# An eight-layer transformer kernel: int8 layer by halves, first steps of the deformable loop reordered, a position split on VectorE, last expert's sums in other PSUM banks

## The chip, the cores and the metric

The kernel runs on one core of a Trainium2 chip. The metric is the device time of one execution in microseconds (us), taken as the median over several executions. The core has TensorE (PE in the profile; PEld is its weight load), VectorE (DVE), ScalarE (ACT), GpSimd (POOL) and SyncE (SP), which issues DMAs. The engines run side by side and meet at semaphores: an instruction can wait for a count, and an instruction can add to one when it has finished. Each engine executes its own instructions in program order. PSUM has 8 banks of 512 fp32 columns on 128 partitions.

## The reference

The input `x` is 16 x 64 tokens of 128 features. Eight residual layers follow each other, each `x = x + layer(layernorm(x))`:

```python
x = x + L0_xattn(...)      # attention over the context, 16 heads
x = x + L0_ffn(...)        # 8 routed and 2 shared SwiGLU experts
x = x + L1_xattn(...)      # channel attention, twice
x = x + L1_ffn(...)        # int8 linear: round(x / x_scale) @ weight_q.T, scaled back, + bias
x = x + L2_xattn(...)      # deformable attention: 5 sampled points for each of 16 heads
x = x + L2_ffn(...)        # 8 experts, 512 wide, top 2, on the first 512 tokens
x = x + L3_xattn(...)      # attention with mask and bias
x = x + L3_ffn(...)        # quantised SwiGLU
```

Three of them matter here. The int8 linear:

```python
x_scale = jnp.maximum(amax, 1e-6) / 127.0
x_q = jnp.clip(jnp.round(x2d / x_scale), -128, 127).astype(jnp.int8)
acc = dot(x_q, weight_q.T)
return acc * x_scale * weight_scale[None, :]     # then + bias
```

The deformable attention computes a position `ix` for each query, head and point (an offset from a linear layer, wrapped by a modulus, rescaled), reads keys and values at `floor(ix)` and `floor(ix) + 1` with weights `1 - dx` and `dx`, and attends over the five points. The expert layer is `h = gelu(x w1[e])`, `y = h w2[e]`, added to each of its tokens with the gate weight of expert e.

## The kernel before, in words

Activations are kept with the tokens on the partitions (`x_tm`, 8 tiles of 128 tokens) and, for matmuls, with the features on the partitions (`h_fm`). Every engine's program is written out by hand, in the order of the calls; nothing reorders it.

**Int8 layer** (`int8_linear`, L1338 on). VectorE first casts the int8 weights and an identity matrix to bf16 (`wq8b`, `ident_b`, L1356, L1357), takes the row maxima of the normed `h_tm`, scales and rounds all 8 tiles, and clips them in one instruction (L1364). TensorE transposes the 8 tiles into bank 4 (L1398), ScalarE copies the whole bank to SBUF (L1424), and TensorE multiplies (L1404). Its result lies in bank 2 (tiles 0 to 3) and bank 3 (tiles 4 to 7). VectorE multiplies each half by the row scales (L1369), by the weight scales (L1374), adds it to `x_tm` (L1375) and takes the statistics of the next layernorm, which is done by halves too (`HalfNorm`: `moments`, `root` on ScalarE, `factors`, then two of four tiles on VectorE and two on ScalarE, `turn` on TensorE, `keep_turned` on ScalarE). Behind the int8 matmuls TensorE has other work in its order: nine transposes of the last layer's weights (L1411), the keys of the last attention (L1415), and fillers (`stay_busy`, L242: matmuls whose result nobody reads), and only then `first_norm.turn`.

**Deformable layer** (`deformable`, L1446 on). TensorE makes queries and offsets for each half. `positions` (L1609 on) turns offsets to positions on 256 columns at a time, and then splits each fp32 position into three bf16 parts (L1636 to L1640), which a one-hot bf16 matmul can move without loss. VectorE does the first of the four blocks, GpSimd the other three one after another. A *unit* is one of four groups of heads in one of two halves of the tokens: 8 units. For each unit `move` (TensorE, 3 matmuls into bank 3) and `keep_positions` (ScalarE) place the positions. Then ten `broadcast`s (two matmuls each, L1744) fill banks 0, 1, 2 in turn; blocks 1, 4 and 7 go to ScalarE (`ramp`, L1833, then `other_side`, L1839) and the other seven to VectorE (`near`, L1906), which writes interpolation weights ("hats"). A broadcast waits until the block three before it has been read. The loop runs over steps w = 0 to 17, two to a unit: `sample(w)` (16 matmuls, L1758) applies the hats of unit w // 2 to keys and values, `to_sbuf` (ScalarE, L1849) copies that out, `turn` (TensorE, L1769) turns it, VectorE multiplies and adds up; `turn_edge` (L1569) and `keep_edge` make the mask of the window's end. During the steps of one unit the hats of the next are made. `spread_q` (ScalarE, L1825) prepares the queries. Ahead of step 0 VectorE also runs `bound_last_keys`, three instructions on the keys of the last attention (L1308 to L1310).

**Experts** (`experts_and_last_attention`). For each expert `up` makes 4 banks of hidden values in banks 0 to 2 in turn, ScalarE applies gelu (L2493), `down(e)` (L2119, 32 matmuls with weight loads) sums into bank 3, and VectorE adds it to `x_tm` with the gate (L2336). Bank 3 is free again after that, so `down(e)` waits for `sum_added`. The last expert uses a bank per tile, in the order 3, 0, 1, 2, and VectorE adds them one at a time (L2347). Then the layernorm of tiles 0 to 3 starts (`late_rows`), with fillers on TensorE ahead of its turn (L367), and its queries go through `guard_queries` (L1289 on) on VectorE before TensorE may start `scores(4)`.

Of the kernel before, what the change touches and what calls it, by code (L numbers as in the profile page):

```python
# [20 lines left out]
P = 128  # L21
B, S, D = 16, 64, 128
T = B * S
NT = T // P
# [91 lines left out]
def build(nc, A, out):  # L116

    ctx = ExitStack()
    with ctx:
# [1042 lines left out]
        def channel_attention(n):  # L1162
# [60 lines left out]
            def _(dve):  # L1223
# [15 lines left out]
                dve.wait_ge(dve_chain, biased)  # L1239
                for k in range(2):  # L1240
# [27 lines left out]
        channel_attention(2)  # L1268

        wq8b = sb("wq8b", [P, P], BF16)
        ident_b = sb("ident_b", [P, P], BF16)

# [28 lines left out]
        def bound_last_keys(dve):  # L1304
# [3 lines left out]
            V.tensor_scalar(nonf, k_fm[:], 0.0, 0.0, ALU.mult, ALU.not_equal)  # L1308
            V.tensor_scalar(h_fm[:], k_fm[:], 0.0, 1e4, ALU.max, ALU.min)
# [28 lines left out]
        def int8_linear(n):  # L1338
# [15 lines left out]
            def _(dve):  # L1354
                dve.wait_ge(rest_in, REST)
                V.tensor_copy(wq8b[:], wq8[:])  # L1356
                V.tensor_copy(ident_b[:], ident)  # L1357
# [27 lines left out]
            def _(pe):  # L1385
                tp = ps[:, 4, :].bitcast(BF16)

# [58 lines left out]
        def deformable(n):  # L1446
            s = lambda name: sem(f"def_{name}")
            q_ps, q_sb, qt_ps, qt_ok, qx_ok = s("q_ps"), s("q_sb"), s("qt_ps"), s("qt"), s("qx")
            off_ps, parts_ok, parts1_ok, mv_ps, ix_ok = s("off_ps"), s("parts0"), s("parts1"), s("moved_ps"), s("ix")
# [85 lines left out]

            MOVE_STEPS = (None, 0, 1, 3, 5, 7, 9, 11)

            def moved(u):  # L1540

# [1351 lines left out]
```

## Time and profile before

| | us |
|---|---|
| median of 3 runs | 464.21 (463.15 to 467.38) |
| the profiled execution, its own time | 463.37 |
| its span, first to last instruction | 461.6 |

| engine | busy us | share of the span | instructions |
|---|---|---|---|
| TensorE | 398.0 | 86% | 3415 |
| VectorE | 359.8 | 78% | 802 |
| ScalarE | 253.0 | 55% | 438 |
| GpSimd | 114.5 | 25% | 97 |

The mean granted clock of TensorE was 0.974 of its full 2.4 GHz. The span lies between the first and the last instruction; the 1.8 us between it and the execution's own time lie around it. A timeline row gives the start, the time taken from the first start to the last end of a group, the engine, the line, the operation with its names and shapes, the count, and, in brackets, how long the engine sat idle before it and what ended that. Instructions of one engine overlap a little, so the start of the next tells more of the pace than the end of the last.

### The profile page before, as it was taken

What the parts mean: (1) busy time and instruction counts of PE and PEld (TensorE: products, weight loads), DVE (VectorE), ACT (ScalarE), POOL (GpSimd) and SP (SyncE); (2) the same over time, 40 slices, a digit from 0 to 9 for tenths busy, and PEclk for the clock granted to TensorE, in tenths of its full rate; (3) what the DMA queues carried; (4) which work ended last, traced back from release to release, by engine and by line L of the source; (5) the groups of instructions that cost most, each with busy time, mean ns of one, the idle gap of its engine ahead of it and who ended that gap; (6) DMA issues with size and microseconds to landing.
All of it is one profiled execution on the core that took longest, in us unless ns stands there. A gap on an engine that the chain in (4) does not pass through costs nothing.

```text
span 461.6 us, 8687 instructions
## 1 busy us (share of the span) xinstructions
PE 398.0 (86%) x3415; PEld 262.4 (57%) x3415; DVE 359.8 (78%) x802; ACT 253.0 (55%) x438; POOL 114.5 (25%) x97
## 2 busy tenths in 40 slices
PE   8988989999999988786787888899999999868156
PEld 5555566566666667553454546385556766643045
DVE  4799646558544587979879898999899689988985
ACT  4785753333223334456797784766766433444942
POOL 3200000006990001005995544031221023100200
PEclk9999999999999999989999999999999999989759
DMA  7890000000000000017000003000000000000001
GB/s 227 357 322 6 1 1 1 1 0 1 0 1 0 1 3 2 0 58 309 2 1 0 3 1 70 0 2 0 2 0 3 1 1 3 1 0 0 1 1 45
DMA packets 11084, 16.51 MB, mean 36 GB/s; under 512 B 5274, under 2 KB 9764, under 8 KB 10148
## 3 DMA queue, kind: packets, MB, share of 16 engines
q1 hardware_dynamic: 10756, 15.17, 9.4%
q10 hardware_dynamic: 288, 0.79, 0.6%
q8 instruction: 27, 0.44, 0.4%
q14 instruction: 13, 0.11, 0.1%
HBM read 15.43 MB, written 0.52 MB: 35 GB/s over the span
## 4 chain that ended last, share of the span: by engine, by line
PE 48%; DVE 32%; ACT 11%; issue 7%; DMA 1%; POOL 0%; ACTq 0%; DVEq 0%
PE ps L852 7%; PE ps L857 7%; PE ps L891 7%; PE ps L2119 4%; PE ps L2109 2%; PE ps L242 2%; DVE arena L1906 2%; DVE stats L252 2%; PE ps L1758 2%; PE ps L2146 1%; DVE arena L610 1%; DVE arena L613 1%; PE ps L2662 1%; DMA ctx_fm<-in_ctx_fm 1%; PE ps L2643 1%
## 5 line engine op out<-in xcount | busy, mean ns | idle before, releaser
L970 DVE SCALAR_TENSOR_TENSOR arena<-ps,cols,arena 128x512 f32<-128x512 f32 x40 | 29.7, 750 | 42.3 <-PE ps L857 38.0
L866 ACT ACTIVATE arena<-ps,cols 128x512 f32<-128x512 f32 x40 | 27.4, 687 | 63.9 <-PE ps L852 63.8
L242 PE MATMUL ps<-const 128*128 128x256 f32 x162 | 43.0, 412 | 7.4 <-ACT arena L2709 4.4
L891 PEld LDWEIGHTS ps<-weights,arena 128*128 128x128 f32 x320 | 38.6, 192 | 8.1 <-issue 8.0
L1906 DVE TENSOR_SCALAR arena<-ps 128x512 f32<-128x512 f32 x56 | 36.4, 683 | 7.3 <-PE ps L1744 3.5
L242 PEld LDWEIGHTS ps<-const 128*128 128x128 f32 x162 | 31.4, 203 | 16.3 <-ACT arena L2709 4.7
L891 PE MATMUL ps<-weights,arena 128*128 128x128 f32 x320 | 39.2, 276 | 0.2 <-DVE x_tm L959 0.2
L857 PE MATMUL ps<-h_fm,weights 128*128 128x512 f32 x80 | 37.7, 593 | 0.7 <-DVE arena L970 0.7
L852 PE MATMUL ps<-h_fm,weights 128*128 128x512 f32 x80 | 37.7, 594 | 0.6 <-ACT h_fm L373 0.6
L2109 PE MATMUL ps<-h_fm,weights 128*128 128x512 f32 x64 | 30.3, 606 | 2.7 <-ACT arena L2493 1.8
L1744 PE MATMUL ps<-l2buf,picks_b 128*128 128x256 bf16 x160 | 25.5, 275 | 6.5 <-DVE arena L1906 4.7
L2119 PEld LDWEIGHTS ps<-weights,arena 128*128 128x128 f32 x256 | 29.4, 192 | 2.6 <-issue 2.6
L2119 PE MATMUL ps<-weights,arena 128*128 128x128 f32 x256 | 30.0, 275 | 0.9 <-DVE x_tm L2336 0.9
L857 PEld LDWEIGHTS ps<-h_fm,weights 128*128 128x128 f32 x80 | 15.1, 190 | 20.2 <-issue 18.2
L1758 PE MATMUL ps<-arena,kexp 128*32 128x320 f32 x256 | 20.5, 438 | 5.3 <-ACT l2buf L1849 3.9
L1065 POOL TENSOR_TENSOR wn<-wn,winv 128x1152 f32<-128x1152 f32 x1 | 2.1, 2129 | 85.7 <-DVE winv L1055 85.7
L2493 ACT ACTIVATE arena<-ps 128x512 f32<-128x512 f32 x32 | 18.0, 597 | 9.2 <-PE ps L2109 9.1
L959 DVE SCALAR_TENSOR_TENSOR x_tm<-ps,arena,x_tm 128x128 f32<-128x128 f32 x80 | 22.4, 342 | 0.3 <-DVE stats L252 0.2
L1744 PEld LDWEIGHTS ps<-l2buf,picks_b 128*128 128x128 bf16 x160 | 12.6, 99 | 17.0 <-DVE arena L1906 10.0
L2109 PEld LDWEIGHTS ps<-h_fm,weights 128*128 128x128 f32 x64 | 11.2, 189 | 17.7 <-issue 10.2
L852 PEld LDWEIGHTS ps<-h_fm,weights 128*128 128x128 f32 x80 | 13.7, 191 | 10.4 <-issue 9.6
L2275 POOL TENSOR_TENSOR arena<-arena 128x1024 f32<-128x1024 f32 x5 | 11.5, 2301 | 31.6 <-DVE arena L2374 31.6
(401 smaller groups left out, 890.8 us busy)
## 6 DMA issues: line engine op xcount, KB each, us to landing
weights<-in_moe_w SPq DMA_DIRECT2D x2, 2048.0 KB, 10.0
weights<-in_moe_w SPq DMA_DIRECT2D x3, 1280.0 KB
l2buf<-in_picks SPq DMA_DIRECT2D x1, 1664.0 KB, 7.9
rows<-in_rows SPq DMA_DIRECT2D x1, 1024.0 KB, 13.7
x_tm<-in_x SPq DMA_DIRECT2D x2, 256.0 KB, 5.2
ctx_fm<-in_ctx_fm ACTq DMA_DIRECT2D x1, 512.0 KB, 5.9
ctx_tm<-in_ctx SPq DMA_DIRECT2D x1, 512.0 KB, 14.5
mats<-in_mats SPq DMA_DIRECT2D x1, 512.0 KB, 14.8
```

The costliest lines, as they stand in the source:

```text
L242: PE.matmul(ps[:, bank, 0:256], ident, const[:, 0:256], start=True, stop=True)
L852: PE.matmul(ps[:, k, :], w1[:, e, P * k:P * k + P], h_fm[:, t], start=True, stop=True)\
L857: PE.matmul(ps[:, 2 + k, :], w2[:, e, P * k:P * k + P], h_fm[:, t], start=True, stop=True)\
L866: AC.activation(silu[:, k, :], ps[:, k, :], ACT.Silu, bias=bias_col(0, e, k)).then_inc(silu_ok, 1)
L891: ins = PE.matmul(ps[:, 4 + u % 2, P * t:P * t + P], glu[:, u % 2, k, P * t:P * t + P], w3[:, e, k, :], start=(k == 0), stop=(k == 1))
L959: ins = V.scalar_tensor_tensor(out=x_tm[:, j], in0=ps[:, 4 + u % 2, P * t:P * t + P], scalar=gates[:, j, e:e + 1], in1=x_tm[:, j], op0=ALU ...
L970: V.scalar_tensor_tensor(out=glu[:, u % 2, k, :], in0=ps[:, 2 + k, :], scalar=bias_col(1, e, k), in1=silu[:, k, :], op0=ALU.add, op1=ALU.m ...
L1744: ins = PE.matmul(ps[:, m % 3, 256 * i:256 * i + 256], picks_b[:, 2 * c + i, :], ixm[:, hg, 256 * half:256 * half + 256], start=True, stop ...
L1758: ins = PE.matmul(ps[32 * hl:32 * hl + 32, 4 + par, 0:NK * S], kvc[:, j, 4 * hg + hl, :], hats[:, u % 2, NK * hl:NK * hl + NK, S * (2 * i ...
L1906: V.tensor_scalar(hat_rows(u, c), ps[:, m % 3, :], 0.0, 1.0, ALU.max, ALU.min).then_inc(near_ok, 1)
L2109: PE.matmul(ps[:, n % 3, :], m2w1[:, e, P * k:P * k + P], h_fm[:, 0:T2], start=True, stop=True)\
L2119: ins = PE.matmul(at_ps, hid[:, e % 2, k, P * j:P * j + P], m2w2[:, e, k, :], start=(k == 0), stop=(k == 3))
```

## The change

1. **Casts.** The casts to `wq8b` and `ident_b` move from the head of the int8 layer into the channel attention ahead of it, in front of VectorE's wait for that layer's result.
2. **Int8 by halves.** The clip, the transposes (now banks 4 and 5), the copy and the waits go by halves of four tiles. The row scales of the second half are applied by ScalarE, in four instructions of one tile each, straight from bank 3.
3. **Table.** The exponential that makes ScalarE load its table moves from behind `keep_positions(0)` to between `keep_turned` and `keep_queries(1)` of the second half.
4. **First steps.** The block-to-bank turn starts at bank 2 instead of 0, with the waits to match. The `move` of unit 1 comes after broadcast 2 (before: in step 0), the `move` of unit 2 inside step 1 before its last two broadcasts (before: at its end). In step 0 the first three broadcasts of the next unit come before `sample(0)`, and `spread_q(0)` after that step's ramps.
5. **Split.** GpSimd computes the third unit's positions but doesn't split them; VectorE splits them at the end of step 0 (new `split_positions`, the five instructions cut out of `positions`).
6. **Last keys.** `bound_last_keys` leaves the place ahead of step 0. Its first instruction goes to the end of step 2, the other two to the end of step 3.
7. **Last expert.** The banks per tile go 0, 1, 2, 3, so only the fourth tile waits for the sum before. The filler ahead of `late_rows.turn` shrinks from 4 to 2.

The diff, cut to its core:

```diff
+                V.tensor_copy(wq8b[:], wq8[:])
+                V.tensor_copy(ident_b[:], ident)
                 for k in range(2):
                     t = slice(4 * k, 4 * k + 4)
                     dve.wait_ge(y_ps, k + 1)
...
-                V.tensor_scalar(xq, t, -128.0, 127.0, ALU.max, ALU.min).then_inc(xq_ok, 1)
+                for k in range(2):
+                    r = slice(4 * k, 4 * k + 4)
+                    V.tensor_scalar(xq[:, r], t[:, r], -128.0, 127.0, ALU.max, ALU.min).then_inc(xq_ok, 1)
...
-                    dve.wait_ge(y_ps, k + 1)
-                    dve_link(V.tensor_tensor(y[:, r], ps[:, 2 + k, :].rearrange("p (j c) -> p j c", j=4),
-                                             over(xs[:, r], 2, D), ALU.mult))
+                    if k == 0:
+                        dve.wait_ge(y_ps, 1)
+                        dve_link(V.tensor_tensor(y[:, r], ps[:, 2, :].rearrange("p (j c) -> p j c", j=4),
+                                                 over(xs[:, r], 2, D), ALU.mult))
                     if k == 1:
                         first_norm.factors(dve)
                         first_norm.apply_on_dve(dve, (0, 1))
+                        dve.wait_ge(xT_ok, 6)
...
-                pe.wait_ge(xq_ok, 1)
-                for j in range(NT):
-                    ins = PE.transpose(tp[:, P * j:P * j + P], xq[:, j], ident_b[:])
-                ins.then_inc(xT_ps, 1)
-                pe.wait_ge(xT_ok, 1)
                 for k in range(2):
+                    pe.wait_ge(xq_ok, k + 1)
+                    tp = ps[:, 4 + k, :].bitcast(BF16)
+                    for j in range(4):
+                        ins = PE.transpose(tp[:, P * j:P * j + P], xq[:, 4 * k + j], ident_b[:])
+                    ins.then_inc(xT_ps, 1)
+                for k in range(2):
+                    pe.wait_ge(xT_ok, k + 1)
...
-                act.wait_ge(xT_ps, 1)
-                AC.activation(xT, ps[:, 4, :].bitcast(BF16), ACT.Copy).then_inc(xT_ok, 1)
+                for k in range(2):
+                    act.wait_ge(xT_ps, k + 1)
+                    AC.activation(xT[:, 512 * k:512 * k + 512], ps[:, 4 + k, :].bitcast(BF16)[:, 0:512], ACT.Copy)\
+                        .then_inc(xT_ok, 1)
+                act.wait_ge(y_ps, 2)
+                for j in range(4, NT):
+                    AC.activation(y[:, j], ps[:, 3, P * (j - 4):P * (j - 4) + P], ACT.Copy, scale=xs[:, j:j + 1])\
+                        .then_inc(xT_ok, 1)
...
                 second_norm.keep_turned(act, 4)
+                AC.activation(warm, const[:, C_BIAS1:C_BIAS1 + 1], ACT.Exp)
                 keep_queries(1)
...
-            MOVE_STEPS = (None, 0, 1, 3, 5, 7, 9, 11)
+            MOVE_STEPS = (None, None, 1, 3, 5, 7, 9, 11)
...
-                positions(pool, G, pool_link, 1, slice(0, 4), parts1_ok)
-                positions(pool, G, pool_link, 0, slice(4, 8), parts1_ok)
-                positions(pool, G, pool_link, 1, slice(4, 8), parts1_ok)
+                positions(pool, G, pool_link, 1, slice(0, 4))
+                for g in range(2):
+                    positions(pool, G, pool_link, g, slice(4, 8))
+                    split_positions(G, pool_link, g, slice(4, 8), parts1_ok)
...
                 for c in range(10):
-                    if c < 2:
-                        pe.wait_ge(qt_ok, c + 1)
+                    if c == 0:
+                        pe.wait_ge(off_sb, 4)
+                    if c in (1, 2):
+                        pe.wait_ge(qt_ok, c)
+                    broadcast(0, c)
                     if c == 2:
-                        pe.wait_ge(off_sb, 4)
-                    broadcast(0, c)
+                        move(pe, 1)
...
-                    if w == 0:
-                        sample(0)
                     if w % 2 == 0 and chunks(w):
                         pe.wait_ge(ix_ok, w // 2 + 2)
                     for c in chunks(w)[:3]:
                         broadcast(w // 2 + 1, c)
+                    if w == 0:
+                        sample(0)
+                    if w == 1:
+                        move(pe, 2)
...
-                bound_last_keys(dve)
...
+                    if w == 0:
+                        dve.wait_ge(third_raw, 1)
+                        split_positions(V, dve_link, 1, slice(0, 4), third_ok)
...
+                    if w == 2:
+                        find_last_keys(dve)
+                    if w == 3:
+                        bound_last_keys(dve)
...
-            SUM_BANK, LAST_BANKS = 3, (3, 0, 1, 2)
+            SUM_BANK, LAST_BANKS = 3, (0, 1, 2, 3)
...
-                    if e >= 1:
-                        pe.wait_ge(sum_added, e)
                     for j in range(4):
+                        if e >= 1 and (j == 3 if e == NE - 1 else j == 0):
+                            pe.wait_ge(sum_added, e)
...
-                stay_busy(pe, 4, 2)
+                stay_busy(pe, 2, 2)
                 late_rows.turn(pe, 0)
```

## Rows read from the trace of the kernel before

**Rows 1.** Page, part 4: the chain that ended last, shares by engine.
```profile
PE 48%; DVE 32%; ACT 11%; issue 7%; DMA 1%; POOL 0%; ACTq 0%; DVEq 0%
```

**Rows 2.** Windows: stretch, busy us (count) by engine, granted clock, DMA.
```profile
197.20:200.70 3.50, 3.50 (x12) 2.47 (x11) 3.33 (x13) 1.45 (x4) 0.00 (x0) 0.51 0.03 7
```

**Rows 3.** Timeline of VectorE, channel attention to int8 layer; columns as explained above.
```profile
182.60 1.40 DVE L1246 TENSOR_TENSOR x_tm<-x_tm,ps 64x512 f32<-64x512 f32 x2 [2.38 <-PE ps L1216]
...
190.12 0.22 DVE L1356 CAST wq8b<-wq 128x128 bf16<-128x128 int32 x1
...
194.07 0.69 DVE L1364 TENSOR_SCALAR arena<-arena 128x1024 bf16<-128x1024 f32 x1
...
197.06 0.69 DVE L1369 TENSOR_TENSOR arena<-ps,arena 128x512 f32<-128x512 f32 x1 [1.16 <-PE ps L1404]
```

**Rows 4.** Timeline of TensorE, int8 layer.
```profile
196.56 0.62 PE L1404 MATMUL ps<-wq8b,arena 128*128 128x128 bf16 x8 [1.12 <-ACT arena L1424]
...
198.75 2.81 PE L1415 MATMUL ps<-ctx_fm,mats 128*128 128x512 f32 x4
...
202.70 0.66 PE L367 MATMUL ps<-const,h_tm 128*128 128x128 f32 x4 [0.27 <-ACT h_tm L349]
```

**Rows 5.** Timeline of ScalarE, int8 layer to the first ramps.
```profile
195.48 1.02 ACT L1424 ACTIVATE arena<-ps 128x1024 bf16<-128x1024 bf16 x1 [2.57 <-PE ps L1398]
...
201.77 0.88 ACT L349 ACTIVATE h_tm<-x_tm,shift,rstd 128x128 f32<-128x128 f32 x2 [0.22 <-DVE shift L341]
...
209.13 0.60 ACT L373 ACTIVATE h_fm<-ps 128x512 f32<-128x512 f32 x1 [0.75 <-PE ps L367]
210.94 0.69 ACT L1592 ACTIVATE q_fm<-ps,cols 128x512 f32<-128x512 f32 x1 [1.22 <-PE ps L1501]
...
213.81 1.28 ACT L1861 ACT_TABLE_LOAD   x1
```

**Rows 6.** Timeline of VectorE, first steps of the deformable loop.
```profile
218.90 0.82 DVE L1308 TENSOR_SCALAR wn<-k_fm 128x1024 int32<-128x1024 f32 x1
...
220.65 1.22 DVE L1310 TENSOR_SCALAR q_fm<-k_fm 128x1024 f32<-128x1024 f32 x1
...
225.98 1.63 DVE L1971 TENSOR_TENSOR x_tm<-x_tm,rows 128x1024 f32<-128x1024 f32 x1
...
237.31 0.69 DVE L1906 TENSOR_SCALAR arena<-ps 128x512 f32<-128x512 f32 x1 [1.31 <-PE ps L1744]
```

**Rows 7.** Timeline of TensorE, first steps of the deformable loop.
```profile
219.93 1.28 PE L1758 MATMUL ps<-arena,kexp 128*32 128x320 f32 x16 [1.37 <-ACT arena L1839]
...
225.72 1.28 PE L1758 MATMUL ps<-arena,kexp 128*32 128x320 f32 x16 [0.42 <-ACT l2buf L1849]
...
228.01 0.67 PE L1569 MATMUL ps<-const,o_fm 128*128 128x80 f32 x4 [0.56 <-ACT l2buf L1586]
```

**Rows 8.** Timelines: the split on VectorE (first, last of five), GpSimd's position steps.
```profile
210.77 0.29 DVE L1636 CAST l2buf<-o_fm 128x256 bf16<-128x256 f32 x1
...
212.09 0.43 DVE L1640 TENSOR_TENSOR l2buf<-o_fm,l2buf 128x256 bf16<-128x256 f32 x1
...
220.25 1.06 POOL L1634 TENSOR_TENSOR ctx_tm<-ctx_tm 128x256 f32<-128x256 f32 x1
...
226.62 1.94 POOL L1623 TENSOR_SCALAR o_fm<-o_fm 128x256 f32<-128x256 f32 x1
```

**Rows 9.** Timelines of ScalarE, VectorE and TensorE around the last expert.
```profile
368.77 0.88 ACT L349 ACTIVATE h_tm<-x_tm,shift,rstd 128x128 f32<-128x128 f32 x2 [0.44 <-DVE shift L341]
...
374.00 0.43 DVE L1289 TENSOR_SCALAR arena<-q_fm 128x512 int32<-128x512 f32 x1 [0.60 <-ACT q_fm L2498]
...
362.77 3.81 PE L2119 MATMUL ps<-weights,arena 128*128 128x128 f32 x32 [0.93 <-DVE x_tm L2336]
...
368.93 1.99 PE L242 MATMUL ps<-const 128*128 128x256 f32 x8
370.76 0.60 PE L367 MATMUL ps<-const,h_tm 128*128 128x128 f32 x4
```

More of the change, by code:

```diff
@@ L1302, in build, with find_last_keys @@
         keys_bounded = []
-        def bound_last_keys(dve):
+        def find_last_keys(dve):
             dve.wait_ge(l3_keys[1], 2)
@@ L1308, in bound_last_keys @@
             V.tensor_scalar(nonf, k_fm[:], 0.0, 0.0, ALU.mult, ALU.not_equal)
+        def bound_last_keys(dve):
             V.tensor_scalar(h_fm[:], k_fm[:], 0.0, 1e4, ALU.max, ALU.min)
@@ L1543, in moved, with wait_parts @@
                 return hg, slice(256 * half, 256 * half + 256)
+            def wait_parts(pe, n):
+                if n == 1:
+                    pe.wait_ge(third_ok, 1)
+                else:
+                    pe.wait_ge(parts1_ok, n - 1)
             def move(pe, u):
                 hg, c = moved(u)
-                edges = sum(step < MOVE_STEPS[u] for step in EDGE_STEPS) if u else 0
+                edges = sum(step < MOVE_STEPS[u] for step in EDGE_STEPS) if u >= 2 else 0
                 if edges:
@@ L1562, in turn_edge @@
             def turn_edge(pe, g):
-                pe.wait_ge(ix_ok, 1 + sum(step < EDGE_STEPS[g] for step in MOVE_STEPS[1:]))
+                pe.wait_ge(ix_ok, 2 + sum(step < EDGE_STEPS[g] for step in MOVE_STEPS[2:]))
                 if g >= 1:
-                    pe.wait_ge(parts1_ok, g)
+                    wait_parts(pe, g)
                 for i in range(2):
@@ L1605, in _, with positions @@
                 second_norm.keep_turned(act, 4)
+                AC.activation(warm, const[:, C_BIAS1:C_BIAS1 + 1], ACT.Exp)
                 keep_queries(1)
                 keep_offsets(1)
-            def positions(eng, E, link, g, pairs, done):
+            def positions(eng, E, link, g, pairs):
                 c = slice(S * pairs.start, S * pairs.stop)
@@ L1633, in positions, with split_positions @@
                     link(E.tensor_tensor(jq(t), jq(t), st, ALU.mult))
-                    link(E.tensor_tensor(o, o, t, ALU.add))
+                    if g == 1 and pairs.start == 0:
+                        E.tensor_tensor(o, o, t, ALU.add).then_inc(third_raw, 1)
+                    else:
+                        link(E.tensor_tensor(o, o, t, ALU.add))
+            def split_positions(E, link, g, pairs, done):
+                c = slice(S * pairs.start, S * pairs.stop)
+                o, t = off[g][:, c], t1[g][:, c]
                 link(E.tensor_copy(parts[g][:, 0, c], o))
@@ L1680, in _ @@
             def _(dve):
-                positions(dve, V, dve_link, 0, slice(0, 4), parts_ok)
+                positions(dve, V, dve_link, 0, slice(0, 4))
+                split_positions(V, dve_link, 0, slice(0, 4), parts_ok)
                 for k in range(2):
@@ L1743, in broadcast @@
                     for i in range(2):
-                        ins = PE.matmul(ps[:, m % 3, 256 * i:256 * i + 256], picks_b[:, 2 * c + i, :],
+                        ins = PE.matmul(ps[:, (m + 2) % 3, 256 * i:256 * i + 256], picks_b[:, 2 * c + i, :],
                                         ixm[:, hg, 256 * half:256 * half + 256], start=True, stop=True)
@@ L1775, in _ @@
                 for c in range(10):
[L1776 to L1777 removed]
+                    if c == 0:
[3 more added lines that the diff above has]
+                    broadcast(0, c)
                     if c == 2:
[L1779 to L1780 removed]
+                        move(pe, 1)
                 pe.wait_ge(kv_ok, 8)
                 for w in range(NW + 2):
[L1783 removed]
+                    if w in MOVE_STEPS[3:]:
                         move(pe, MOVE_STEPS.index(w))
@@ L1798, in _ @@
                         sample(w)
-                    if w == 1:
-                        move(pe, 2)
                     if w == 14:
@@ L1860, in _ @@
                 keep_positions(act, 0)
-                AC.activation(warm, const[:, C_BIAS1:C_BIAS1 + 1], ACT.Exp)
                 for c in ACT_BLOCKS:
                     ramp(0, c)
+                    if c == ACT_BLOCKS[0]:
+                        keep_positions(act, 1)
                 for c in ACT_BLOCKS:
@@ L1866, in _ @@
                 for w in range(NW + 2):
-                    if w in MOVE_STEPS[1:] and w != 1:
+                    if w in MOVE_STEPS[3:]:
                         keep_positions(act, MOVE_STEPS.index(w))
-                    if w == 0:
-                        spread_q(0)
                     if w in EDGE_STEPS:
```

21 lines of the change are left out of this document (10 added, 11 removed).

## The prediction

> **What bounds the kernel now.** I read the page's chain first, then the timelines of each engine over the three places the diff touches, then the windows for the granted clock. By the chain TensorE sets 48% of the span, VectorE 32%, ScalarE 11%, DMA 1% [rows 1]: no engine bounds the whole, it is a relay. So an edit is worth what it takes out of the handoffs on the chain at its place, and everything behind a shortened handoff moves forward as one, as long as nothing from outside (a DMA, GpSimd) is met. I therefore follow one mark through each place: how much earlier does it happen?
>
> **Casts and clip.** The two casts stand between `h_tm` and the row maxima. The first starts at 190.12 [rows 3] and the pair held VectorE up by about 0.15. In the channel attention VectorE sits idle 2.38 ahead of 182.60 [rows 3], so 0.4 of casts is covered there; without that cover it would cost its 0.4. Behind L1246 nothing else waits for them. The clip of 1024 columns takes 0.69 [rows 3]; half of that plus a fixed part is about 0.42, so the first half is ready 0.27 sooner.
>
> **Int8 relay.** The copy of the whole bank on ScalarE takes 1.02 [rows 5]; 512 columns take 0.60 (L373 [rows 5]), 0.42 less. The eight matmuls or transposes take 0.62 [rows 4] at a pace of 0.06, so four transposes are done 0.23 sooner. Sum for L1369 of the first half: 0.15 + 0.27 + 0.23 + 0.42 = 1.07 earlier, 196.0 instead of 197.06. The second half follows 0.5 behind on ScalarE, and its four scalings are new: two instructions of 128 columns with two operands from memory take 0.88 (L349 [rows 5]), so four take 1.7. They run from about 196.4 to 198.1, while VectorE still adds the first half, and the weight copies behind them on ScalarE still finish by 199.6, when the `root` is wanted. On VectorE they save 0.7. By VectorE and ScalarE alone the normed half would be ready 1.3 earlier.
>
> TensorE is what is late next. Its fixed work (L1411, L1415, fillers) starts behind the last int8 matmul: 196.0 + 0.23 instead of 196.56 + 0.45, which is 0.78 earlier, and it ended 0.27 before `first_norm.turn` [rows 4]. So the turn comes 0.78 + 0.27 = 1.05 earlier: **1.05** is the gain of this part.
>
> The clock bears on it. From 197.2 to 200.7 the granted clock was 0.51, the lower level of 1.2 GHz, after TensorE had been idle for 1.12 of the time just before [rows 2, 4]; the four passes of L1415 took 2.81. With halves TensorE waits less there. If the clock stays up, TensorE is ready over 1 us sooner and the turn is bound by ScalarE, at 1.3 instead of 1.05. I take 1.05 and keep 0.25 for the range.
>
> **Table load.** The load takes 1.28 at 213.81 [rows 5], ahead of the first ramp. Its new place is the 1.22 in which ScalarE waits before L1592 [rows 5]. With the warm exponential it overhangs by 0.2, and TensorE's own queries cover that. It takes about 0.7 off the first ramp, which else waits for its broadcast. The Trainium skill (ScalarE: Activation LUTs, What ACT_TABLE_LOAD costs) adds a drain of 1.38 us to the load; by that the overhang would be 1.6 and nearly all the benefit gone, but here the next instruction starts right behind the 1.28.
>
> **First steps.** I walked the ten broadcasts, the seven hats (about 0.61 apart) and the three ramps forward by their waits, starting 1.0 earlier than before. ScalarE's `other_side`s end at 218.3, so `sample(0)` starts at 218.35 against 219.93 [rows 7]: 1.6 earlier. VectorE has no `bound_last_keys` ahead of step 0; it ran from 218.90 to about 221.8 [rows 6], 2.8 of work, in front of the hats that `sample(1)`'s banks waited for. With three broadcasts ahead of `sample(0)` only the fourth hat waits, till about 220.0. Then comes the split: the five instructions took 1.75, 210.77 to 212.52 [rows 8], and the raw positions are there in time: GpSimd starts 1.05 earlier, and its add ended at 221.31 [rows 8], so 220.3 at the latest.
>
> What does the split cost beside a busy GpSimd? The trace has VectorE instructions on SBUF at that time: 1024 columns take 0.82 and 1.22 [rows 6] where 0.69 is normal [rows 3], 1.4 times on average. Lower bound: 1.75. Upper: each of the five waits for one GpSimd step, 1.94 the longest [rows 8]. I take 1.4 times, 2.4. This is the rule of the Trainium skill that speaks against the change (SBUF — State Buffer, SBUF: two separate sides): VectorE and GpSimd take turns at one pair of ports, and who comes second stands still for the whole instruction; its worst is rival D.
>
> Behind the split wait the hats of step 1, `move(2)` and broadcasts 18 and 19. Walked on: the last of these hats starts at about 224.8, `sample(1)` at 224.5 against 225.72, and, since `move(2)` no longer stands between it and the edge, `turn_edge(0)` at 225.8 against 228.01 [rows 7]. That is **2.2 earlier**, 1.05 of which came from the int8 layer. x_tm's bias add (L1971, 1.63 [rows 6]) then ends at about 227.1, in time for the multiply that waits for the turn behind broadcast 20.
>
> **Last keys.** The first instruction (0.8) at the end of step 2 falls into waits of VectorE and delays two hats by 0.2, with no effect on `sample(3)`, which waits for ScalarE. The other two (2.1) at the end of step 3 meet an idle of 1.31 before 237.31 [rows 6], so the next hat is 1.0 late with the 0.2. Its broadcast successor has 0.5 of slack; `sample(4)` gets 0.5 later. From there VectorE is tight, so it stays: **0.5 back**. The bounds are 0 and the whole 2.9. The loop leaves 2.2 - 0.5 = **1.7** earlier. GpSimd, rid of one split, is further ahead of need than before, and no DMA bounds the loop (1% of the chain [rows 1]).
>
> **Last expert.** `down(7)` waited 0.93 for the sum before it [rows 9]. Three of its tiles need not; the fourth comes long after it. The whole tail is 0.93 earlier. Then the layernorm: TensorE did four fillers from 368.93 to 370.76 [rows 9], 0.46 each, and the normed tiles were there at 368.77 + 0.88 = 369.65 [rows 9], so the filler held up the turn. With two it is at 368.93 - 0.93 + 0.92 = 368.92, 1.84 earlier. The guard on VectorE started at 374.00 after an idle of 0.60 [rows 9]; its own queue allows 0.93 + 0.60 less a gap, so **1.5** earlier. `scores(4)` waits for that guard. Nothing on the way to the end is bound from outside.
>
> **Sum.** 1.7 + 1.5 = 3.2. The profiled execution took 463.37, so 460.2 by its own account. The median of the runs is 464.21, 0.84 above; the same 3.2 from it gives **461.0** (0.7% less). One per cent is 4.6 us, and that is what a measurement of this kernel can tell from no change.
>
> **Rivals.**
> *A, as summed:* 461.0, chance 0.50. Its own range is 459.9 to 462.0.
> *B, the clock stays up and the ports hardly meet:* 0.25 more in the int8 layer, 0.65 for the split, and 0.5 if the two last-key instructions are hidden wholly, 1.4 in all: 459.6; with the four passes of L1415 and the loop's dense start a little less again, 459.0. For it: idle of TensorE shrinks [rows 4], GpSimd's steps are short beside VectorE's. Against: 0.82 and 1.22 in the rows [rows 6]. Chance 0.27.
> *C, the moved work is paid in full:* the last keys cost 2.9 instead of 0.5, because VectorE has no slack once the start is tight: 2.4 back, 463.4. Against: the idle of 1.31 [rows 6]. Chance 0.15.
> *D, slower:* the split queues behind GpSimd at each step. GpSimd then runs the first steps of its next block, with the 1.94 among them [rows 8]. If the five together take 1.75 + 5 x 1.0 = 6.8 instead of 2.4, 4.4 are lost: 465.4. It decides from a split of 5.6 on, where the 3.2 are gone. At five times 1.94, 11.5 for the split, it would be 470.1. The rule named above is this one at its worst. Against: the 0.82 and 1.22 of the two instructions [rows 6] are at most 0.53 over normal. Chance 0.08.
>
> **How the numbers follow.** The range takes A and B, and of C all but its end: 459.0 to 463.4. Faster by over 1% means under 459.6: B's greater part and the low end of A, 0.28. Slower by over 1% means over 468.8, only the far end of D and what I overlooked: 0.05. The rest, 0.67, is within 1%.
>
> **What would show it.** Right: L1369 near 196.0 and the first turn (L367) near 201.7; no table load ahead of the first ramp; `sample(0)` near 218.4, `turn_edge(0)` near 225.8; the split under 3; VectorE without idle ahead of the first hat of step 4; `down(7)` without wait, the second-last turn near 368.9 less the loop's gain, and the guard 1.5 earlier beyond the loop's gain. Wrong: a split over 4, idle of VectorE ahead of it (raw positions late), `sample(4)` less than 1 earlier than before, or TensorE at 0.5 of its clock in a stretch of the loop where it was at 1.00.

## The result, and the profile after

The kernel after takes **461.32 us** (median of 20 runs, 459.6 to 466.37); the kernel before, run beside it, 466.04 (20 runs, 463.15 to 469.25). The ratio is 0.9907, with a 95% interval of 0.988 to 0.9933. The predicted 461.0 us is close, but part of that is cancellation: one step failed, and two terms, the int8 layer and the tail, were larger than I made them. A ratio below leaves out executions more than 1.5% above the fastest of their own kernel, which takes 5 of the 12 of parts 1 to 6 and 3 of the 12 of the loop with fillers and none elsewhere; medians and mean clocks are of all executions. The ratios follow the means more than the medians, so they are not the quotients of the medians shown. The profiled execution of after took 460.47, span 458.4, so 2.9 and 3.2 less than that of before.

The marks of the prediction, as starts in the two traces (us):

| mark | before | after | distance from the mark above: before, after |
|---|---|---|---|
| `x_tm` add of the channel attention | 182.60 | 182.32 | |
| first turn of the normed half (L367) | 202.70 | 201.11 | 20.10, 18.79 |
| `sample(0)` | 219.93 | 217.96 | 17.23, 16.85 |
| `sample(1)` | 225.72 | 224.11 | 5.79, 6.15 |
| `turn_edge(0)` | 228.01 | 226.29 | 2.29, 2.18 |
| `sample(4)` | 238.95 | 238.25 | 10.94, 11.96 |
| `keep_last_values`, behind the loop | 291.60 | 290.66 | 52.65, 52.41 |
| `down(7)` | 362.77 | 360.72 | 71.17, 70.06 |
| its layernorm's turn (L367) | 370.76 | 367.79 | 7.99, 7.07 |
| guard of the queries (L1289) | 374.00 | 371.20 | 3.24, 3.41 |
| end of the span | 461.6 | 458.4 | 87.60, 87.20 |

So between the two traces the int8 layer gives 1.31, the deformable loop from the turn to `keep_last_values` takes back 0.65 (88.90 to 89.55), and the tail gives 1.86. The rest, 0.28 ahead of the first changed line and 0.40 behind the guard, lies where nothing was changed.

The chain of after, from the page, against [rows 1]: still a relay, no engine carries it alone.

```profile
PE 47%; DVE 34%; ACT 10%; issue 7%; DMA 1%; POOL 0%; ACTq 0%; DVEq 0%
```

**Int8 layer.** Timeline of VectorE after; L1366, L1372 are the L1364, L1369 of [rows 3]:

```profile
179.93 0.18 DVE L1241 CAST wq8b<-wq 128x128 bf16<-128x128 int32 x1
...
182.32 0.68 DVE L1249 TENSOR_TENSOR x_tm<-x_tm,ps 64x512 f32<-64x512 f32 x1 [2.07 <-PE ps L1216]
...
193.73 0.77 DVE L1366 TENSOR_SCALAR arena<-arena 128x512 bf16<-128x512 f32 x2
...
195.81 0.69 DVE L1372 TENSOR_TENSOR arena<-ps,arena 128x512 f32<-128x512 f32 x1 [0.18 <-PE ps L1408]
```

Timelines of ScalarE and TensorE after, against [rows 4, 5]:

```profile
194.65 1.08 ACT L1429 ACTIVATE arena<-ps 128x512 bf16<-128x512 bf16 x2 [2.02 <-PE ps L1402]
196.22 1.15 ACT L1433 ACTIVATE arena<-ps,arena 128x128 f32<-128x128 f32 x4 [0.49 <-PE ps L1408]
...
195.30 0.88 PE L1408 MATMUL ps<-wq8b,arena 128*128 128x128 bf16 x8 [0.35 <-ACT arena L1429]
...
197.01 1.88 PE L1419 MATMUL ps<-ctx_fm,mats 128*128 128x512 f32 x4
...
201.11 0.66 PE L367 MATMUL ps<-const,h_tm 128*128 128x128 f32 x4 [1.35 <-ACT h_tm L349]
```

The casts sit in an idle that is still 2.07 long. The first half comes nearly as predicted: L1372 at 195.81 where 196.0 was forecast, and 0.97 earlier behind the `x_tm` add, where 1.07 was. TensorE has less idle (0.35 where [rows 4] had 1.12), its four passes take 1.88 and not 2.81, and it now waits 1.35 for ScalarE ahead of the turn.

**First steps of the loop.** Timeline of TensorE after, against [rows 7]: steps 0 and 1.

```profile
217.96 1.28 PE L1786 MATMUL ps<-arena,kexp 128*32 128x320 f32 x16 [0.43 <-ACT arena L1869]
...
222.68 0.49 PE L1574 MATMUL ps<-v,picks_b 128*128 128x256 bf16 x3 [1.72 <-DVE v L1666]
...
224.11 2.25 PE L1786 MATMUL ps<-arena,kexp 128*32 128x320 f32 x16
226.29 1.15 PE L1587 MATMUL ps<-const,o_fm 128*128 128x80 f32 x4
```

`move(2)` (L1574) waits 1.72 for the split on VectorE. The `sample(1)` behind it takes 2.25 where `sample(0)` took 1.28. The windows (stretch, busy us and count of TensorE, its weight loads, VectorE, ScalarE, GpSimd, then granted clock and DMA) say why:

```profile
220.00:224.00 4.00, 1.70 (x12) 0.76 (x11) 3.90 (x9) 4.00 (x8) 3.59 (x6) 1.00 0.00 0
224.00:228.00 4.00, 4.00 (x27) 2.15 (x26) 2.12 (x4) 1.46 (x4) 3.84 (x4) 0.57 0.02 4
```

The granted clock is 0.57 from 224 to 228, mostly at the lower level of 1.2 GHz, behind 4 us in which TensorE was busy for 1.70. In before it was 1.00 over this stretch and low in the int8 layer instead [rows 2].

The split, timeline of VectorE after, against [rows 8]:

```profile
220.21 0.28 DVE L1662 CAST v<-ctx_tm 128x256 bf16<-128x256 f32 x1
220.53 0.50 DVE L1663 TENSOR_TENSOR ctx_tm<-ctx_tm,v 128x256 f32<-128x256 f32 x1
...
221.81 0.72 DVE L1666 TENSOR_TENSOR v<-ctx_tm,v 128x256 bf16<-128x256 f32 x1
```

From 220.21 to 222.53 are 2.32, forecast 2.4. No idle stands ahead of it (its row has no bracket): the raw positions are there in time.

The last keys, timeline of VectorE after, against [rows 6]:

```profile
234.90 1.02 DVE L1312 TENSOR_SCALAR h_fm<-k_fm 128x1024 f32<-128x1024 f32 x1
235.84 1.21 DVE L1313 TENSOR_SCALAR q_fm<-k_fm 128x1024 f32<-128x1024 f32 x1
236.97 0.68 DVE L1937 TENSOR_SCALAR arena<-ps 128x512 f32<-128x512 f32 x1
```

The 1.31 of idle ahead of the hat in [rows 6] is filled.

**Last expert.** Timeline of TensorE after, against [rows 9]: `down(7)`, the two fillers (four matmuls; the four of before were eight), the turn.

```profile
360.72 3.74 PE L2156 MATMUL ps<-weights,arena 128*128 128x128 f32 x32
...
366.82 1.13 PE L242 MATMUL ps<-const 128*128 128x256 f32 x4
367.79 0.60 PE L367 MATMUL ps<-const,h_tm 128*128 128x128 f32 x4
```

`down(7)` has no wait where [rows 9] had 0.93.

### The profile page after: what moved, and what is told of

It is laid out like the page before. It is cut to its first block, busy times and chain, and to the rows that moved or that the text cites. A ratio compares the mean times of both kernels' runs of the same rounds, so it can differ in the third digit from the quotient of the medians.

```text
span 458.4 us, 8682 instructions
## 1 busy us (share of the span) xinstructions
PE 396.8 (87%) x3411; PEld 260.9 (57%) x3411; DVE 360.2 (79%) x807; ACT 253.6 (55%) x443; POOL 111.7 (24%) x92
## 4 chain that ended last, share of the span: by engine, by line
PE 47%; DVE 34%; ACT 10%; issue 7%; DMA 1%; POOL 0%; ACTq 0%; DVEq 0%
PE ps L852 7%; PE ps L857 7%; PE ps L891 7%; PE ps L2156 5%; DVE arena L1937 3%; PE ps L2146 2%; PE ps L1786 2%; DVE stats L252 2%; DVE arena L2405 1%; DVE arena L2402 1%; DVE arena L610 1%; DVE arena L613 1%; PE ps L242 1%; DMA ctx_fm<-in_ctx_fm 1%; DVE arena L2433 1%
## 5 line engine op out<-in xcount | busy, mean ns | idle before, releaser
L1786 PE MATMUL ps<-arena,kexp 128*32 128x320 f32 x256 | 21.5, 455 | 3.7 <-ACT l2buf L1879 2.6
L2530 ACT ACTIVATE arena<-ps 128x512 f32<-128x512 f32 x32 | 18.0, 597 | 9.2 <-PE ps L2146 9.1
L1863 ACT ACTIVATE arena<-ps 128x512 f32<-128x512 f32 x24 | 14.4, 599 | 8.8 <-PE ps L1772 8.8
```

Of the source, the lines that this page charges most:

```text
L1786: ins = PE.matmul(ps[32 * hl:32 * hl + 32, 4 + par, 0:NK * S], kvc[:, j, 4 * hg + hl, :], hats[:, u % 2, NK * hl:NK * hl + NK, S * (2 * i ...
```

## Experiments

What is to be settled: whether the terms have the sizes that the prediction gave them; whether the wait for the split and the low clock behind it are what the loop lost; and whether GpSimd lengthens the split. The rival to the second is that the last keys (rival C) or the new order itself cost the loop its gain. In the lists below, the distance from the `x_tm` add to `keep_last_values`, the int8 layer and the loop together, is called the **front**: 109.00 in before, 108.34 in after.

### The tail alone

The kernel before, with part 7 of the change (and, in the second run, its banks without the shorter filler):

```diff
-            SUM_BANK, LAST_BANKS = 3, (3, 0, 1, 2)
+            SUM_BANK, LAST_BANKS = 3, (0, 1, 2, 3)
...
-                stay_busy(pe, 4, 2)
+                stay_busy(pe, 2, 2)
```

> The kernel before with part 7 alone (banks 0, 1, 2, 3 for the last expert, 2 fillers instead of 4). Theory (the two waits in the tail add up, as the two traces show them): the last expert starts 0.9 to 1.1 earlier, the guard behind the layernorm 1.5 to 1.9 earlier; 1.7 us faster, ratio 0.996. Rival (the tail is bound by something that comes back later, such as a low granted clock once there are fewer fillers): under 0.5 us.

> The kernel before with the new banks for the last expert, all 4 fillers kept. Theory: the sum's wait is worth 0.93 to 1.1 us by itself and the two fillers the other 0.6 to 0.8, so about 1.0 us faster. Rival: the turn is set by ScalarE and the fillers cost nothing, so the same as with 2 fillers, 1.7 us.

Whole part: ratio 0.996 (0.9929 to 0.999), median 463.39. Banks alone: 0.9978 (0.9947 to 1.001), median 465.08. The kernel before, in the series of this and the next two sections, had a median of 464.21 and a mean of 465.36 (35 runs), so for the banks alone the timing shows no gain. TensorE in the trace of the whole part, with VectorE's guard, then TensorE with the banks alone (without its `down(7)`, at 365.78):

```profile
361.63 3.74 PE L2119 MATMUL ps<-weights,arena 128*128 128x128 f32 x32
...
367.72 1.13 PE L242 MATMUL ps<-const 128*128 128x256 f32 x4
368.69 0.60 PE L367 MATMUL ps<-const,h_tm 128*128 128x128 f32 x4
...
372.10 0.42 DVE L1289 TENSOR_SCALAR arena<-q_fm 128x512 int32<-128x512 f32 x1
```

```profile
371.87 1.99 PE L242 MATMUL ps<-const 128*128 128x256 f32 x8
373.70 0.60 PE L367 MATMUL ps<-const,h_tm 128*128 128x128 f32 x4
```

From `down(7)` to the turn it is 7.06 with two fillers and 7.92 with four, 7.99 in before. From `keep_last_values` to the guard: 82.40 before, 80.55 with the part (361.63, 368.69 and the guard at 372.10, `keep_last_values` at 291.57), 81.22 with the banks alone. So the part is worth **1.85**, 1.18 of it the banks. The turn gains 0.86 by two fillers less, but the guard only 0.67: it starts 3.41 behind the turn instead of 3.24, and the idle of 0.60 ahead of it [rows 9] is gone, so now VectorE's own queue holds it. The 1.85 agrees with the timed 0.4% (1.9 us).

### The int8 layer alone

The kernel before, with parts 1 and 2 of the change (casts, halves):

> The kernel before with the casts moved and the int8 layer by halves (parts 1 and 2). Theory: the first turn of the layernorm comes 1.05 us earlier at the low granted clock, 1.3 with the clock up, and all of it is carried to the end: 1.0 to 1.3 us faster. Rival (the low clock only moves to a later stretch, where TensorE is on the path): 0 to 0.5 us.

Ratio 0.9985 (0.9955 to 1.0015), median 464.27. In the trace the first turn comes 18.79 behind the `x_tm` add, against 20.10: **1.31** earlier, and the front is 107.66, so 1.34 shorter, with nothing lost on the way to `keep_last_values`. Whether it reaches the end is not shown: the timing can't resolve 1.3 us (0.28%), and in this trace the stretch behind the guard is 1.4 longer than in before. The distance was 20.08 to 20.10 in each of the five traces without this part and 18.78 or 18.79 in each of the nine with it, whatever the rest of the kernel did. The clock's part is told by the banks-only kernel above, whose int8 layer is that of before and lies 4.2 later in its trace. The window that answers to [rows 2] there:

```profile
201.40:204.90 3.50, 3.50 (x17) 2.12 (x15) 3.33 (x13) 1.34 (x4) 0.00 (x0) 1.00 0.02 7
```

The clock was 1.00 where before had 0.51, and the distance was 20.08 all the same. The low clock of [rows 2] cost nothing, since VectorE and ScalarE set the turn.

### The loop alone

The kernel before, with parts 3 to 6 of the change (table, first steps, split, last keys):

> The kernel before with parts 3 to 6 (table, first steps, split, last keys). By my prediction the loop's share is 2.2 - 1.05 - 0.5 = 0.65 us faster. Theory of the moved clock stretch: in the trace after, TensorE fell to 0.5 of its clock at 224 to 227.6 us, behind an idle of 1.7 us that the split causes; without the int8 part the phase differs, so between 0.3 slower and 1.5 faster. Rival (VectorE is the bound of the loop): no gain, whatever the clock.

Ratio **1.0044** (1.0012 to 1.0076), median 466.76 against 464.21: slower, where my sum said 0.65 gained. TensorE in steps 0 and 1, then the window behind it:

```profile
219.38 1.28 PE L1779 MATMUL ps<-arena,kexp 128*32 128x320 f32 x16 [0.44 <-ACT arena L1862]
...
224.10 0.59 PE L1567 MATMUL ps<-v,picks_b 128*128 128x256 bf16 x3 [1.71 <-DVE v L1659]
...
225.74 2.26 PE L1779 MATMUL ps<-arena,kexp 128*32 128x320 f32 x16
```

```profile
224.00:228.00 4.00, 3.90 (x24) 1.16 (x24) 3.63 (x5) 2.36 (x5) 3.75 (x5) 0.57 0.02 4
```

The same idle and the same clock as in after. The front is 109.67, 0.67 longer, though `sample(0)` comes 0.38 sooner behind the turn. `sample(1)` then follows 6.36 behind it instead of 5.79, which takes that back, and between `turn_edge(0)` and `sample(4)` another 0.89 goes, to the last keys in this trace. Their two bounds on VectorE:

```profile
236.36 1.18 DVE L1312 TENSOR_SCALAR h_fm<-k_fm 128x1024 f32<-128x1024 f32 x1
237.46 1.10 DVE L1313 TENSOR_SCALAR q_fm<-k_fm 128x1024 f32<-128x1024 f32 x1
```

### Fillers in step 1, GpSimd made to wait, and both

Two edits to the kernel after: three fillers (six matmuls) ahead of `move(2)`, so that TensorE works while the split runs; and GpSimd kept from its next block of positions until the split has ended.

```diff
                     if w == 1:
+                        stay_busy(pe, 3, 7)
                         move(pe, 2)
...
                 positions(pool, G, pool_link, 1, slice(0, 4))
+                pool.wait_ge(third_ok, 1)
```

> The changed kernel with 3 fillers on TensorE in step 1, ahead of move(2), where it stood idle for 1.72 us; nothing else differs. Theory (the idle lowers the granted clock in the stretch behind it in most executions, which costs 1 to 1.8 us there): the stretch at 224 to 228 us shows a granted clock of 1.00, turn_edge(0) comes about 1 us earlier than in the trace after, and the ratio falls by 0.002 to 0.004 below that of the changed kernel (0.9907). Rival (the clock there costs nothing, because VectorE is what the loop waits for): the same 0.9907.

> The changed kernel with GpSimd waiting until VectorE has finished the split, before it starts its next block. Theory (the split's 2.3 us instead of 1.75 come from GpSimd working at the same time): the split takes 1.7 to 1.8 us, everything up to sample(1) is 0.4 to 0.5 us earlier, GpSimd's later blocks end 2.5 to 3 us later and nobody waits for them; 0.3 to 0.5 us faster. Rival (the split is slow because of its own chain or of ScalarE): it stays at 2.3 us and nothing changes.

> Both: 3 fillers in step 1 and GpSimd waiting for the split. If both theories hold, 1.3 to 2 us faster than the changed kernel: ratio 0.987. The fillers (1.5 us) might then be longer than the shortened idle (1.2 us), which would give 0.3 back.

The fillers: 0.9878 (0.9841 to 0.9915), median 460.46. TensorE in their trace:

```profile
220.97 1.46 PE L242 MATMUL ps<-const 128*128 128x256 f32 x6
222.85 0.49 PE L1574 MATMUL ps<-v,picks_b 128*128 128x256 bf16 x3 [0.41 <-DVE v L1666]
...
224.28 1.28 PE L1786 MATMUL ps<-arena,kexp 128*32 128x320 f32 x16
225.50 0.67 PE L1587 MATMUL ps<-const,o_fm 128*128 128x80 f32 x4
```

`move(2)` starts where it started (4.72 behind `sample(0)` in both), for the split is as long, but the idle is 0.41, `sample(1)` takes 1.28 and the edge comes 1.22 behind it instead of 2.18. The front is 106.33, 2.0 shorter than in after. About half of that, 0.96, is won ahead of the edge. Another 1.02 comes between the edge and `sample(4)` (10.94, 11.96 in after): 0.67 ahead of the first hat of step 2, and 0.35 because the two bounds on the last keys took 0.74 and 0.88 there, not 1.02 and 1.21.

GpSimd's wait: 0.9888 (0.9842 to 0.9934), median 460.46. VectorE in its trace, then TensorE:

```profile
221.92 0.28 DVE L1662 CAST v<-ctx_tm 128x256 bf16<-128x256 f32 x1
222.24 0.42 DVE L1663 TENSOR_TENSOR ctx_tm<-ctx_tm,v 128x256 f32<-128x256 f32 x1
...
223.22 0.42 DVE L1666 TENSOR_TENSOR v<-ctx_tm,v 128x256 bf16<-128x256 f32 x1
...
223.79 0.49 PE L1574 MATMUL ps<-v,picks_b 128*128 128x256 bf16 x3 [1.13 <-DVE v L1666]
```

The split takes **1.72** (221.92 to 223.64), the lower bound of the prediction (1.75), and the clock stays at 1.00 behind an idle of 1.13. Here another stretch was low, 0.58 from 208 to 212, ahead of the first hat: the way from the second turn to that hat took 7.45, against 5.95 in after. That puts the front at 107.55.

Both: 0.9866 (0.9834 to 0.9899), median 459.68. Its window over the disputed stretch:

```profile
224.00:228.00 4.00, 3.76 (x37) 2.30 (x35) 3.44 (x5) 3.39 (x8) 3.73 (x4) 1.00 0.00 0
```

The front is 106.07, 2.93 shorter than before and 2.27 shorter than after: the whole loss of the loop is gone, and 1.6 are won there. The median is the lowest of all, beside 465.4 of before in this series. But the intervals of all three versions overlap that of after (0.988 to 0.9933), so the timing doesn't show a gain over it.

### The last keys

The kernel after, with all three instructions on the last keys on 64 of 1024 columns. It leaves out the bounds of the other 960, so it is not a replacement:

```diff
-            V.tensor_scalar(h_fm[:], k_fm[:], 0.0, 1e4, ALU.max, ALU.min)
+            V.tensor_scalar(h_fm[:, 0:64], k_fm[:, 0:64], 0.0, 1e4, ALU.max, ALU.min)
```

> The changed kernel with the three instructions of the last keys' bounds on 64 instead of 1024 columns (left out: the bounds of the other 960, so this part of the keys' guard is not computed), which takes their 2.9 us nearly away. Theory (VectorE has slack at the end of step 2 and 1.3 of slack at the end of step 3): 0.5 us faster than the changed kernel. Rival C of the prediction (the moved work is paid in full): 2.4 us faster. Other rival (all hidden): no change.

Ratio 0.9932 (0.9899 to 0.9966), median 461.99: no gain over after. Timeline of VectorE:

```profile
236.71 0.30 DVE L1312 TENSOR_SCALAR h_fm<-k_fm 128x64 f32<-128x64 f32 x1
236.94 0.18 DVE L1313 TENSOR_SCALAR q_fm<-k_fm 128x64 f32<-128x64 f32 x1
238.16 0.69 DVE L1937 TENSOR_SCALAR arena<-ps 128x512 f32<-128x512 f32 x1 [1.05 <-PE ps L1772]
```

The time saved turns into 1.05 of idle ahead of the same hat. From the first hat of step 2 to `sample(4)` it is 9.96, as in before and with the fillers; in after it is 10.31 and in the loop alone 10.84. So the last keys cost nothing where their two instructions ran at 0.74 and 0.88, 0.35 where they took 1.02 and 1.21, and 0.88 in the loop alone, where the first of the three was long too (1.18). A second trace of after (below) has the same marks as this one up to this place, and its front is 109.68 against 109.70 here: in it the last keys, at 0.68 and 0.88, cost nothing. Rival C, with 2.9 in full, falls. Why the instructions are long in some traces was not tested by itself. This trace also repeats the low clock: 0.69 from 224 to 228.

### Do the parts add up?

The loop alone with the fillers; parts 1 to 6 of the change together; and, timed once more in the same series, the kernel after and the version with both edits:

> Parts 3 to 6 alone on the kernel before, with the 3 fillers in step 1. Parts 3 to 6 alone were 2.0 us slower (ratio 1.0044) at a mean granted clock of 0.963 instead of 0.967. Theory (the idle of TensorE in step 1 is the whole reason): the mean clock rises to 0.967 or more and the kernel is 0.7 to 1.5 us faster than before, ratio 0.997 to 0.9985. Rival (VectorE's new work, or something else in the order, makes the loop longer whatever the clock): it stays at 1.003 to 1.005.

> Parts 1 to 6 without part 7. Theory of a plain sum: 0.9907 of the whole less the 0.004 of the tail, so 0.9947. Theory that the parts don't add, as int8 alone (0.9985) and the loop alone (1.0044) give 1.003 together: 1.003.

> The changed kernel itself, on the chip and in the rounds of the others of this call: 0.9907 again within 0.003, mean granted clock 0.968.

> The changed kernel with fillers and with GpSimd waiting for the split, a second time: 0.9866 again within 0.003, 1.3 to 2 us under the changed kernel of this call. If it is within 0.5 us of the changed kernel, the first result was the spread between executions.

The kernel before stood at 466.77 here (23 runs, mean 466.23). The fourth column divides the mean of all executions by that mean.

| kernel | ratio (95%) | median us | ratio of all executions | mean granted clock |
|---|---|---|---|---|
| loop alone with fillers | 0.9974 (0.9933 to 1.0016) | 466.76 | 0.9998 | 0.965 |
| parts 1 to 6 | 0.994 (0.9901 to 0.9979) | 465.03 | 0.9991 | 0.965 |
| after | 0.9866 (0.9826 to 0.9905) | 460.79 | 0.9875 | 0.970 |
| after with both edits | 0.9871 (0.9832 to 0.991) | 460.87 | 0.9880 | 0.969 |

In the first two rows the two ratios differ, for the reason given with the result. By all executions both kernels are level with the kernel before, within about 0.004.

Two results went against me. The fillers did not make the loop alone faster than before; its traced execution (469.34, the longest of its 12) lost clock elsewhere, 0.70 from 208 to 212, and its front was 111.62. And the version with both edits did not beat after in this series, though its front was 106.05 in the trace, the same as in the first, while that of after was 109.68. VectorE and TensorE in this second trace of after:

```profile
221.82 0.54 DVE L1662 CAST v<-ctx_tm 128x256 bf16<-128x256 f32 x1
222.39 0.90 DVE L1663 TENSOR_TENSOR ctx_tm<-ctx_tm,v 128x256 f32<-128x256 f32 x1
...
224.79 0.49 PE L1574 MATMUL ps<-v,picks_b 128*128 128x256 bf16 x3 [2.22 <-DVE v L1666]
...
226.44 2.36 PE L1786 MATMUL ps<-arena,kexp 128*32 128x320 f32 x16
```

The split took 2.83 here and the idle was 2.22. The table sets the 14 traces side by side. The column "low clock at" tells where the granted clock of a 2 us window was under 0.95, in us behind the `x_tm` add; the windows cover 8 to 58 behind it. The trace of parts 1 to 6 is of the longest of its 12 executions too (469.3).

| traces | idle ahead of `move(2)` | split | second turn to first hat | low clock at | front |
|---|---|---|---|---|---|
| before, tail alone | none | | 5.84 | 14 to 18 | 109.00, 108.93 |
| banks alone, int8 alone | none | | 5.84 | nowhere | 108.91, 107.66 |
| after | 1.72 | 2.32 | 5.95 | 42 to 46 | 108.34 |
| loop alone | 1.71 | 2.33 | 5.95 | 14 to 18, 42 to 46 | 109.67 |
| after again, short last keys, parts 1 to 6 | 2.22 | 2.83 | 7.44 | 26 to 30, 42 to 48 | 109.68, 109.70, 109.88 |
| after with fillers | 0.41 | 2.31 | 5.95 | nowhere | 106.33 |
| after with GpSimd's wait | 1.13 | 1.72 | 7.45 | 26 to 30 | 107.55 |
| after with both, twice | none | 1.73 | 5.95 | nowhere | 106.07, 106.05 |
| loop alone with fillers | 0.93 | 2.83 | 7.45 | 22 to 26, 28 to 34 | 111.62 |

Three things are read from it. All five traces with the new first steps and neither edit have an idle of 1.7 or more ahead of `move(2)` and a low clock from 42 on; none of the five with an edit has either, nor the four with the old steps. That link is shown: the two edits touch the idle by different ways, and each takes the low clock away. A low clock at 26 to 30 goes with about 1.5 more ahead of the first hat, where TensorE has the queries, the offsets and the broadcasts in its order. (In the last row a low clock at 22 to 26 also goes with 7.34 instead of 5.74 from the first turn to the second.) And it carries on: GpSimd's block starts 28.68 behind the `x_tm` add in both traces of after, but the split starts 9.21 behind GpSimd in the first and 10.71 in the second, so it meets other steps of GpSimd. In all traces without GpSimd's wait it took 2.31 to 2.33 at 9.2 behind and 2.83 at 10.7.

What stays open is how much of it the median sees. Executions of one kernel differ by up to 8.5 us (6.8 for after), and the mean granted clock goes with it: after lay between 459.6 and 466.37, the slowest at a mean clock of 0.960, the traced one at 0.974. Further stretches behind the loop vary too: from the guard to the end it is 86.94 to 87.60 in nine traces and 88.10 to 88.97 in the other five. Six runs of each version don't separate a gain of 2 us from that. Nor is it settled whether the parts add: 0.9985 and 1.0044 give 1.003. Parts 1 to 6 together measured 0.994, which is 0.009 apart with about 0.006 of uncertainty on the difference, but by all executions 0.9991, which is 0.004 apart and within it. With the tail's 0.996 that would make 0.995 for the whole, where 0.9907 was measured, again within the uncertainty. Whether the int8 part changes how often the clock falls behind it was not tried.

## Why the prediction was right, and where it was wrong

**Int8 layer: mechanism right, 1.31 instead of 1.05.** The first half came within 0.1 of the forecast by its distance from the `x_tm` add. The step that was off is "TensorE is what is late next". The 0.27 of idle ahead of the turn in [rows 4] already said that TensorE was waiting for ScalarE in before, and with the clock at 1.00 it got there 1.35 early. So the figure for VectorE and ScalarE, 1.3, holds, rival B's part in this place. None of the nine traces with halves has a low clock there, so whether it would be 1.05 with one is not shown. The four scalings took 1.15, not 1.7: I priced them by instructions with two operands from memory, and these have one; that this is the reason is argued, not shown.

**Table load: hidden.** ScalarE after:

```profile
208.16 1.28 ACT L1624 ACT_TABLE_LOAD   x1
209.45 0.20 ACT L1624 ACTIVATE v<-const 128x1 f32<-128x1 f32 x1
```

The next instruction starts 0.01 behind the 1.28, and in before it starts at 215.10, 0.01 behind its load too. The drain of 1.38 us that the Trainium skill adds (ScalarE: Activation LUTs, What ACT_TABLE_LOAD costs) does not show in either. The next waiting step, the first hat, came 5.95 behind the second turn against 5.84, so at most 0.1 was overhang. The first ramp came 30.69 behind the `x_tm` add instead of 32.61, which is 0.61 earlier beyond the int8 layer's 1.31, where about 0.7 was forecast.

**First steps: right up to `sample(0)`, wrong from there.** `sample(0)` came at 217.96, forecast 218.35. The walk then had `sample(1)` at 224.5 and `turn_edge(0)` at 225.8; they came at 224.11 and 226.29. The failed step is the sentence "behind the split wait the hats of step 1, `move(2)` and broadcasts 18 and 19". I listed who waits, and priced the lateness of each, but not the clock behind TensorE's idle. `sample(1)` started about when forecast and then ran at close to half the rate: 2.25 instead of 1.28, and the turn of the edge 1.15 instead of 0.67 [rows 7]. The 0.65 that the loop should have gained became a loss of 0.65 in the trace, 0.67 in the loop alone. In the loop alone not all of it is the clock: the last keys took 0.88. The last paragraph of the prediction names this sign (0.5 of the clock in a stretch that was at 1.00) without giving it a price or a chance; it was the most important rival and was missing. A second of its signs of being wrong came up too: `sample(4)` was to be at least 1 earlier than before and was 0.70.

**Split: right in the first trace of after, 2.32 for 2.4; 2.83 in the second.** It is 1.72 with GpSimd halted, so GpSimd's work beside it costs 0.6 to 1.1 in five instructions. The factor of 1.4 was also a little off its own rows: 0.82 and 1.22 for 0.69 average to 1.48, which makes 2.6. In direction the traces agree with the rule weighed there (the Trainium skill, SBUF — State Buffer, SBUF: two separate sides); in the second trace of after one instruction grew by 0.48 (L1663, 0.90 for 0.42). That the ports are the reason is argued; the run shows only that GpSimd's work is. Rival D, at 5.6 and more, falls.

**Last keys: 0.35 in the first trace of after, 0 in the second, 0.88 in the loop alone; forecast 0.5.** Rival C, at 2.9, falls; the bounds given, 0 and 2.9, hold.

**Tail: 1.85, forecast 1.5.** The banks gave 1.18 at the guard, not 0.93. The term that was too small is the 0.93: `down(7)` came 1.10 sooner, 0.17 more than the idle that was removed (a start behind a wait takes a little itself, which is argued and not shown), and the guard 0.08 more. The fillers gave the other 0.67, 0.07 more than the 0.60 of idle that I counted.

**The sum.** 1.31 - 0.65 + 1.85 = 2.5 from changed lines in the trace, forecast 3.2. The trace's own 3.2 includes 0.7 from elsewhere. The timed difference is 4.7 between the medians, 4.3 by the ratio. The gap from 2.5 to 4.3 is not explained by one pair of traces, so over a third of the timed gain has no cause shown here: the traced execution of before, 463.37, lay at the low end of its 463.15 to 469.25. I took 464.21 as the level of before from three runs; with more it was 466.04 here, and 464.21, 465.4 and 466.77 in the three series of experiments. So the 461.0 is near the measured 461.32 partly because the level was too low and the gain too small by a like amount.

## What to carry to other kernels

When a reorder makes TensorE wait for something new, price two things: the wait, and the instructions behind it at the lower clock; if they are on the path, a few filler matmuls in the gap are worth a try. A stretch at a low clock costs only where TensorE sets the pace, so look at who ends the wait at its end before giving its removal a price. Test parts of a change one by one: here, by the traces, the parts at either end carried the gain, and the middle, which had most of the diff, was a loss by itself.

## What the hardware did that was not expected

- Where the clock falls is not fixed by the program alone. In two traces of the same kernel (after) the stretch at 26 to 30 behind the `x_tm` add was once at 1.00 and once at 0.58.
- A low clock was free in the int8 layer: 20.10 from add to turn at 0.51, 20.08 at 1.00.
- An idle of 1.13 ahead of `move(2)` left the clock at 1.00; behind idles of 1.71 to 2.22 it fell, in all five traces that had them. Where between them it turns, and whether the idle's length alone decides, was not measured.
- A VectorE subtraction of 256 columns between two SBUF operands (L1663) took 0.42 with GpSimd halted and 0.50 and 0.90 beside it.
- The same five instructions took 2.32 or 2.83 according to when they met GpSimd's steps, 9.2 or 10.7 behind the start of its block.
